# Node steps of a graph kernel: ScalarE normalises the newer step's rows before it copies the turned rows

## The reference

```python
x = _layernorm(x + _L0_gnn_ref(x, edge_index, W, attn, W_out))                  # attention, 4 heads of 64
x = _layernorm(x + _L1_gnn_ref(x, edge_attr_64, edge_index, W_edge, W_n2m, ...)) # attention, message width 128
...
# inside the second layer, per node
m = x @ W_n2m.T
x_r = m @ Wskip.T + bskip
beta = sigmoid(concat([out, x_r, out - x_r]) @ Wbeta.T)
return (beta * x_r + (1 - beta) * out) @ W_m2n.T
```

## Time and profile before

| What | Value |
|---|---|
| Three runs | 1257.87, 1260.95, 1261.74 us; median 1260.95 |
| Profiled execution: its own time | 1271.05 us |
| Profiled execution: span from first to last instruction | 1269.3 us |
| TensorE matmuls busy | 1174.8 us, 93% of the span |
| VectorE busy | 1041.8 us, 82% |
| ScalarE busy | 829.2 us, 65% |
| GpSimd busy | 851.0 us, 67% |
| Mean granted TensorE clock | 0.978 |
| ScalarE's normalisations (line 722) | 142 instructions in 71 steps, 76.7 us busy |

### The profile page before, as it was taken

One profiled execution on the slowest core, in us unless ns is written; L12 is line 12 of the kernel. 1 busy time (PEld: TensorE's weight loads), 2 busy tenths in 40 slices (PEclk: granted clock), 3 DMA queues, 4 the chain that ended last, 5 costly groups with the idle time before them and its releaser, 6 DMA issues.

```text
span 1269.3 us, 28496 instructions
## 1 busy us (share of the span) xinstructions
PE 1174.8 (93%) x6990; PEld 1024.3 (81%) x6990; DVE 1041.8 (82%) x3799; ACT 829.2 (65%) x2787; POOL 851.0 (67%) x1076
## 2 busy tenths in 40 slices
PE   2899999999998689999999899999999996899995
PEld 2788999988896578788788699989999995688884
DVE  2767776777778799999999889999999987788985
ACT  0366666665666866666666856666665668689996
POOL 6688888888883455555554677767677743278887
PEclk9899999999999899999999999999999998899998
DMA  7578888888884477788877787777777742555652
GB/s 210 164 224 284 270 268 257 270 268 266 262 265 132 134 254 249 244 267 249 259 253 238 220 255 217 217 223 221 206 220 223 224 136 78 158 189 187 185 188 96
DMA packets 208795, 276.99 MB, mean 218 GB/s; under 512 B 40044, under 2 KB 140419, under 8 KB 208633
## 3 DMA queue, kind: packets, MB, share of 16 engines
q1 hardware_dynamic: 187913, 223.83, 56.0%
q0 software_dynamic: 19264, 50.85, 13.5%
q10 hardware_dynamic: 1456, 0.49, 0.2%
HBM read 159.67 MB, written 117.12 MB: 218 GB/s over the span
## 4 chain that ended last, share of the span: by engine, by line
PE 58%; DVE 17%; issue 12%; POOL 7%; ACT 3%; DMA 1%; another core or an unknown queue 1%; SPq 1%; DVEq 0%; POOLq 0%; ACTq 0%
PE banks L751 19%; PE banks L864 7%; PE banks L741 6%; PE banks L1422 4%; POOL out L1577 4%; PE banks L854 3%; PE banks L1254 3%; POOL output_r L1583 3%; DVE AT L1280 3%; PE banks L866 2%; PE banks L1409 2%; PE banks L1427 2%; PE banks L953 2%; PE banks L1247 2%; DVE node_X L777 2%
## 5 line engine op out<-in xcount | busy, mean ns | idle before, releaser
L751 PE MATMUL banks<-m_ext,node_XT 128*128 128x257 f32 x1568 | 376.0, 382 | 0.0
L751 PEld LDWEIGHTS banks<-m_ext,node_XT 128*128 128x128 f32 x1568 | 284.6, 192 | 33.0
L777 DVE SCALAR_TENSOR_TENSOR node_X<-banks,node_be,node_X 128x256 f32<-128x256 f32 x392 | 169.4, 474 | 79.5 <-ACT node_be L703 53.6
L678 POOL TENSOR_TENSOR node_r<-node_vv,half 128x4 f32<-128x4 f32 (+1 forms) x202 | 212.8, 1053 | 17.1 <-POOL node_vv L673 0.3
L709 ACT ACTIVATE node_XT<-banks 128x512 f32<-128x512 f32 x196 | 117.5, 599 | 131.7 <-PE banks L741 126.9
L673 POOL TENSOR_SCALAR node_vv<-node_mv 128x4 f32<-128x4 f32 (+1 forms) x202 | 56.5, 279 | 190.3 <-DVE node_mv L785 173.7
L716 ACT ACTIVATE node_sq<-node_X 128x256 f32<-128x256 f32 x392 | 158.0, 409 | 1.2 <-DVE node_X L777 1.2
L770 DVE BATCH_NORM_STATS2 node_st<-node_X 128x6 f32<-128x256 f32 x392 | 145.4, 412 | 1.3 <-issue 0.5
L690 ACT ACTIVATE node_X<-node_X,node_r 128x256 f32<-128x256 f32 x326 | 146.0, 497 | 0.0
L741 PE MATMUL banks<-ident,node_X 128*128 128x128 f32 x784 | 122.0, 279 | 19.0 <-issue 11.9
L831 POOL DMA_INDIRECT ring<-in_x,src_col x100 | 106.8, 1068 | 26.5 <-issue 14.4
(11 more groups left out here) (270 smaller groups left out, 2740.8 us busy)
## 6 DMA issues: line engine op xcount, KB each, us to landing
node_X<-in_x SPq DMA_DIRECT2D x196, 256.0 KB
out<-node_X SPq DMA_DIRECT2D x196, 256.0 KB
ring<-rows SPq DMA_DIRECT2D x210, 128.0 KB
rows<-ring SPq DMA_DIRECT2D x100, 256.0 KB
rows<-ring SPq DMA_DIRECT2D x200, 128.0 KB
MB<-keeps SPq DMA_DIRECT2D x40, 320.0 KB, 4.5
store<-rows SPq DMA_DIRECT2D x90, 128.0 KB
MB<-picks SPq DMA_DIRECT2D x50, 128.0 KB
```

The costliest lines, as they stand in the source:

```text
L678: pool.tensor_tensor(r[:, s % 4, NT * lo:NT * hi], v, self.c.half[:, NT * lo:NT * hi], ALU.pow).then_inc(self.roots, 1)
L751: last = pe.matmul(ps[:, NT * o + k, 0:D + 1], self.XT[:, o, k * D + h * P:k * D + (h + 1) * P], c.m_ext[:, h, :], start=(h == 0), stop=(h ...
L777: last = dve.scalar_tensor_tensor(out=X[:, n % U, k, :], in0=ps[:, b + k, 0:D], scalar=self.be[:, n % 4, k:k + 1], in1=X[:, n % U, k, :], ...
```

## The change

In `Nodes.scalar` the normalisation of node s-2, with its wait for the shift, is moved from behind the squares to ahead of the copy of the turned rows. It stays behind the sigmoid. Everything else is as it was.

```diff
                 act.activation(self.be[:, n % 4, :], c.psum[:, b:b + NT, D], ACT.Sigmoid).then_inc(self.beta_ready, 1)
+            if live(s, 2, NSTEPS) and self.normed_by[s - 2] == "A":
+                n = s - 2
+                act.wait_ge(self.shifts, self.normed_by[0:n + 1].count("A"))
+                for k in range(NT):
+                    last = act.activation(X[:, n % U, k, :], X[:, n % U, k, :], ACT.Identity, bias=self.nb[:, n % 4, k:k + 1], scale=self.r[:, (n + 1) % 4, k:k + 1])
+                last.then_inc(self.x1_act, 1)
             if live(s, 3, NSTEPS):
                 n = s - 3
...
                 last.then_inc(self.squared, 1)
-            if live(s, 2, NSTEPS) and self.normed_by[s - 2] == "A":
-                n = s - 2
-                act.wait_ge(self.shifts, self.normed_by[0:n + 1].count("A"))
-                for k in range(NT):
-                    last = act.activation(X[:, n % U, k, :], X[:, n % U, k, :], ACT.Identity, bias=self.nb[:, n % 4, k:k + 1], scale=self.r[:, (n + 1) % 4, k:k + 1])
-                last.then_inc(self.x1_act, 1)
             if live(s, 8, NSTEPS) and self.scaled_by[s - 8] == "A":
                 self.scale(act, s)
```

## The result

| | before | after |
|---|---|---|
| Median of eight runs each | 1259.41 us | 1264.75 us (1262.83 to 1266.19) |
| Ratio, 95% interval | 1 | 1.0036 [1.0026, 1.0047] |
| Profiled execution: its own time, span | 1271.05, 1269.3 us | 1265.1, 1263.3 us |
| TensorE matmuls, ScalarE busy | 1174.8, 829.2 us | 1171.9, 836.1 us |
| ScalarE's normalisations waiting for the shift, whole span | 1.8 us, once | 72.0 us, 50 times |

The kernel became slower by 0.36%, 4.5 us of 1260. The forecast was 3.67 us and 1264.6; the time is in its range. The ratio stands just above the 0.3% that I called the bound of what can be told, and its interval reaches to both sides of it.

What follows compares the result with a forecast made beforehand. TensorE was taken to bound the gather and message stages, ScalarE the first softmax. Terms 1.29 + 0.98 + 0.41 + 0.29 + 0.70 = 3.67 us, on the 1260.95 us median, gave 1264.6; range 1260 to 1268.5.

Steps and rivals of the forecast that it cites:

- ScalarE's waits for the shift: Sign: ScalarE's normalisation waits for the shift in most steps that have one, and the copy follows it at once.
- gather's first masks: Sign at the gather's start: its first masks load about 2.3 us later; if not later, the first two terms are wrong.
- The exponentials: First softmax: copy and squares come after the wait for the shift, delaying exponentials and the sigmoid VectorE awaits: +1.29 us.
- The second hold: First softmax, shift ending at 433.47 after eight softmax operations: delays the copy of sums, a sigmoid and VectorE's update, +0.98 us.
- Entry of the gather: Shift ending at 443.73 makes ScalarE 1.20 us late; VectorE's update moves from 446.69 to 447.10, +0.41 us.
- Entry of the messages: Shift ending at 717.81 after a late GpSimd: ScalarE 0.81 us late, VectorE's update at 721.18 for 720.89, +0.29 us.
- Second softmax: Two holds of ScalarE, 0.35 and 1.14 us; TensorE's transposes also wait for the late copy, 1062.35 for 1061.61: +0.70 us.
- Gather and messages at 0: Both long stages: TensorE sets the pace and 2.8 us of cover hide the later copy: 0, lower bound -1 us.
- TensorE waited for the copy: Sign in the gather: if TensorE waits for the copy, the 2.8 us cover was misread and the loss far larger.
- (a): Rival: VectorE's softmax chain, not ScalarE, releases what follows, so the delay is absorbed; time 1261, chance 0.2.
- (b): Rival: normalised rows reach TensorE earlier, removing its idle time in both softmaxes: about 6 us faster, 1255, chance 0.08.
- (c): Rival: TensorE's pause lengthens in the first softmax, two more node steps at low clock add 2.7 us: 1267.3, chance 0.15.

Runs made afterwards that it cites:

- softmaxes alone: Kernel before, with the normalisation ahead of the copy only for nodes 74 to 84 and from 191 (the two softmax stretches): 1.0030 [1.0020, 1.0040].
- extra transposes: Changed kernel plus 20, 36 and 12 unread identity transposes after the products of steps 78, 79 and 196: 1.0023; the kernel before with the same: 0.9986.
- messages alone: Kernel before, with the normalisation ahead of the copy only for nodes 146 to 190, end of gather to near the end of the messages: 0.9986 [0.9975, 0.9997].
- gather alone: Kernel before, with the normalisation ahead of the copy only for nodes 85 to 145, beside the gather: 0.9999 [0.9989, 1.0010].
- early shift: VectorE's shift moved to the end of the step before: all steps, changed kernel 0.9971, kernel before 1.0011; softmaxes only, with new order there, 0.9954.
- again: The kernel before, unchanged, run and profiled a second time: 1261.14 against 1261.08 us, 0.9997 [0.9988, 1.0006].

## Why the prediction was right, and where its sum was off

*Where the loss is.* Right. The softmaxes alone cost 1.0030 [1.0020, 1.0040]; their four terms with the gather's entry, 1.29 + 0.98 + 0.41 + 0.70 = 3.38 us, lie in that interval (2.5 to 5.0 us). Of the signs that I had named, ScalarE's waits for the shift came (50, in 71 steps), and the gather's first masks were issued 3.27 us later by the offset (432.10 for 438.72), where I had said about 2.3; the rest is the copy of sums, below.

*The exponentials, +1.29.* The trace of after has +1.28 to +1.29, the other kernels with this hold +1.27 (softmaxes alone, from the update before) and +1.28 (extra transposes). It goes on to VectorE undiminished, as predicted.

*The second hold, +0.98.* Between the copy of sums and the update: 3.28 - 2.28 = 1.00; 1.01 and 0.99 in the two other kernels.

*Entry of the gather, +0.41.* 3.74 - 3.28 = 0.46, and 0.46 with the softmaxes alone.

*Entry of the messages, +0.29.* From the shift of the earlier trace rows to the update, 5.02 less 4.81 = 0.21, and 0.22 in the kernel with the messages alone. It can't be seen in a time by itself.

*Second softmax, +0.70.* 3.54 - 2.82 = 0.72 at the transposes, and 0.73 and 0.72 in the two other kernels. In after another 0.89 follows, because the eight products took 3.58 us, half clock, where line 751 otherwise takes 1.90. The kernel with the softmaxes alone has the same order there and not this loss (4.61 for 4.64), so the order alone doesn't bring it.

*Gather and messages at 0.* For the gather the times agree (0.9999 [0.9989, 1.0010]). The traces say otherwise: from the update at its entry to that at the messages' entry the three with the new order there and the late shift lose 1.3 (after), 1.1 (gather alone) and 3.1 us (extra transposes), 0.2 of it in the first and third the hold at the messages' entry, while the seven experiments with the old order and the late shift there lie between -0.6 and +0.3. A loss of 1.1 us would still fit the interval of the time, so whether this term is really 0 stays open, and so does what would cause it. As predicted, TensorE waited for the copy nowhere in 450 to 700. For the messages the term was mis-sized: I had a lower bound of -1, the part alone measured -1.8 [-3.2, -0.4], and the four traces with the new order and the late shift throughout this stage gain between 0.8 and 2.4 us from the update at its entry to the transposes at its end. But the kernel with the early shift in the softmaxes and the old order here gains 0.7 as well, and adding the new order here to it changed nothing in the time. What this stage gains, and why, is open.

*The sum.* 3.67 predicted, 4.5 [3.3, 5.9] measured: the two can't be told apart. The terms of the holds are each within 0.1 us. That the total came as near as this is in part luck. The trace of after ends 3.94 us late; 1.29 + 1.00 + 0.46 + 0.72 = 3.47 of it are the holds, and five moves that the sum did not have nearly cancel: +0.99 at the copy of sums, +1.34 in the gather (0.21 of it the hold at the messages' entry), -2.26 in the messages, +0.89 in the second softmax and -0.49 behind it. The 0.99 stands at transposes that took 0.85 us, where the kernel before has 0.51 for the same four (at 428.07). Three more profiles with the order of before at this place have +0.48 (again), +0.80 (gather alone) and 0.00 (messages alone), so most of it may be chance of the clock.

*The rivals.* (a) Absorbed: no, each hold reached VectorE or TensorE in full. (b) Faster, because the rows reach TensorE sooner: in the second softmax's first step they do (1046.14 for 1054.16, 8.0 us earlier where the trace is 7.1 ahead), in its second not (1053.54 for 1060.43, 6.9 earlier). TensorE waits for the copy instead, 8.4 us in the first softmax, as I had argued against it. The view calls the wait of 0.77 us in the earlier trace rows issue; that it is a wait for the rows follows from the earlier trace rows, where they end at 1061.51, 0.10 us ahead of the transposes. My reason against this rival, that ScalarE has nothing to spare, I had read in the first softmax. In the second, where these waits stand, ScalarE works 13.67 of 16 us:

```profile
1050.00:1066.00 16.00, 13.21 (x75) 10.82 (x74) 12.20 (x39) 13.67 (x46) 5.84 (x9) 1.00 0.17 66
```

The Trainium skill (Perfetto Trace Analysis, Optimization Strategies) asks for the engine that blocks TensorE to be made faster. The traces agree with it there, once the shift is early too: with the new order the waits ahead of the last four groups of transposes are 0, 0, 0.74 and 0.39 us, with the old one 0.33, 0.77, 0.77 and 0.59 at either place of the shift. So the rival failed on a wait which a different edit could take away. (c) The clock: granted 0.71 from 404 to 420 in after, 0.68 from 414 to 430 in before and 0.79 from 404 to 420 in its second profile, so the pauses are not colder beyond chance. The transposes then gave the same to both orders, as far as intervals of some 1.3 us to each side can tell, so this is a cost that the kernel had before the change. TensorE: Matmul & The Clock Gate (Part 1) of the Trainium skill says that activity releases the throttle on the clock; the trace agrees with its 0.89 under the extra transposes.

*The chances.* I gave 0.52 to no change and 0.40 to slower, since my sum stood at 3.7 of a bound of 3.8. The measured loss of 4.5 has that bound inside its interval, so this one result doesn't say which of the two chances was the better. What the sum lacked is not a hold that I had missed: it is TensorE's half clock in two places, which I had carried as a rival with other numbers, and what the long stages gain and lose.

## What to carry to other kernels

On an engine that works in order, moving an instruction forward moves its wait forward, over everything that is now behind it. The price can be read from the old trace: end of what it waits for, plus the work that it overtakes, less its old start; in the five stretches priced so it came true to 0.1 us. It prices the wait alone, and not what the long stages make of the move, here 1 to 2 us either way. Before giving the move up, look at what is late: here the awaited instruction was 0.13 us long and stood behind 2.3 us of softmax operations that it doesn't need, and moving both turned a loss of 0.30% into a gain of 0.46%. And a repair that helps the changed kernel proves nothing on the change until it has been tried on the old one; for the fastest kernel here that was not done.

## What the runs showed that I had not expected

68 extra transposes, whose result nothing reads, did not make either kernel slower: by the ratios they were 0.13 and 0.14% faster, the second just clear of none. From 404 to 420 the granted clock was 0.89 where it is 0.71 in the new order and 0.79 in the old one without them, and in the new order a group of transposes on the softmax's chain went from 0.85 to 0.51 us.

The early shift at all steps gives the old order nothing in the time (1.0011) and the new one 0.65% (from 1.0036 to 0.9971). In the old order the trace has the exponentials 2.0 us earlier and nothing of it at the end of the messages (+1.59). Why the gain is lost on the way was not settled; the waits for GpSimd's roots, 1.8 us in the messages, are a candidate.

A long wait can change its name without growing. With the squares behind the normalisation and the copy ahead of it, the waits name ScalarE for 80.7 us of GpSimd's idle time in the gather; the idle time itself is 117.4 us for 114.7. That order cost as much in all as the full move (1.0035), though it leaves TensorE's copy in its place, and where it does so outside the softmaxes is open.
